# Four transformer layers on one core: layer 1's query product split 3 to 13 heads, and two small steps of each norm moved to VectorE

## The reference

```python
def _layernorm(x, axis=-1, eps=1e-05):
    m = jnp.mean(x, axis=axis, keepdims=True)
    v = jnp.var(x, axis=axis, keepdims=True)
    return (x - m) / jnp.sqrt(v + eps)
...
inter = jnp.einsum('bnchd,bnhde->bnche', q, KVcum)
den_inter = jnp.einsum('bnchd,bnhd->bnch', q, Kcum)
scores = jnp.einsum('bnchd,bnkhd->bnhck', q, k)
scores = jnp.where(mask, scores, 0.0)
intra = jnp.einsum('bnhck,bnkhe->bnche', scores, v)
den_intra = jnp.transpose(jnp.sum(scores, axis=-1), (0, 1, 3, 2))
out = (inter + intra) / (den_inter + den_intra + ATT_EPS)[..., None]
```

## Time and profile before

| | |
|---|---|
| median of 3 runs | 1859.21 us (1857.06 to 1859.85) |
| the profiled execution | 1858.92 us, of which the span of instructions is 1857.1 us |
| PE busy | 1768.9 us, 95% |
| POOL busy | 1273.5 us, 69% |
| DVE busy | 1238.0 us, 67% |
| ACT busy | 1091.2 us, 59% |
| granted TensorE clock | 0.994 of full |

### The profile page before, as it was taken

How to read it: one execution, slowest core, us unless ns; L and a number is a source line. 1 busy time by engine, 2 the same in 40 slices (tenths; PEclk the granted TensorE clock), 3 DMA queues, 4 the chain that set the end, 5 groups by cost and what they waited for, 6 DMA issues and landing times.

```text
span 1857.1 us, 31831 instructions
## 1 busy us (share of the span) xinstructions
PE 1768.9 (95%) x10270; PEld 1340.9 (72%) x10270; DVE 1238.0 (67%) x4307; ACT 1091.2 (59%) x2684; POOL 1273.5 (69%) x1779
## 2 busy tenths in 40 slices
PE   8999999989999999999999899999999999999998
PEld 5788998665666567657665577777778887888874
DVE  7953235687769876887789655543466756768774
ACT  6563225656886578667876676564345556544456
POOL 6665558998879987997899884341356755554465
PEclk9999999999999999999999999999999999999999
DMA  6200000010000000000000000000000001000002
GB/s 237 77 11 1 1 2 4 1 47 1 1 1 1 1 1 1 1 1 1 1 1 1 5 5 5 1 7 1 2 4 1 1 23 26 18 1 1 1 7 63
DMA packets 24473, 26.44 MB, mean 14 GB/s; under 512 B 3492, under 2 KB 21284, under 8 KB 23924
## 3 DMA queue, kind: packets, MB, share of 16 engines
q1 hardware_dynamic: 24308, 24.41, 4.1%
HBM read 22.26 MB, written 2.15 MB: 13 GB/s over the span
## 4 chain that ended last, share of the span: by engine, by line
PE 69%; POOL 14%; DVE 7%; ACT 5%; issue 4%; DMA 0%; POOLq 0%; SPq 0%; DVEq 0%; ACTq 0%
PE ps L86 63%; POOL arena L103 13%; PE ps L89 6%; ACT arena L97 4%; DVE arena L103 2%; DVE arena L109 1%; DVE arena L106 1%; POOL arena L106 1%; DVE arena L126 1%; DVE arena L141 1%; ACT L97 1%; DVE arena L123 0%; DVE arena L129 0%; DVE arena L112 0%; ACT arena L98 0%
## 5 line engine op out<-in xcount | busy, mean ns | idle before, releaser
L103 POOL TENSOR_TENSOR arena<-arena 128x512 f32<-128x512 f32 (+6 forms) x796 | 734.5, 937 | 298.9 <-DVE arena L103 146.5
L97 ACT ACTIVATE arena<-ps 128x128 f32<-128x128 f32 (+9 forms) x1100 | 368.6, 369 | 445.1 <-PE ps L86 337.8
L86 PE MATMUL ps<-arena 128*128 128x128 f32 (+4 forms) x2864 | 465.1, 296 | 25.8 <-DVE arena L103 12.8
L86 PEld LDWEIGHTS ps<-arena 128*128 128x128 f32 x2864 | 380.0, 192 | 118.0 <-issue 47.5
L103 DVE TENSOR_TENSOR arena<-ps,arena 128x128 f32<-128x128 f32 (+4 forms) x680 | 295.0, 446 | 239.3 <-PE ps L86 227.4
L97 ACT ACTIVATE arena<-arena 128x128 f32<-128x128 f32 (+1 forms) x772 | 300.0, 442 | 45.8 <-POOL arena L103 41.3
L97 ACT ACTIVATE arena<-ps,cols 128x512 f32<-128x512 f32 x324 | 216.9, 689 | 170.2 <-PE ps L86 158.1
L86 PE MATMUL ps<-arena,cst 128*128 128x360 f32 (+1 forms) x768 | 294.0, 498 | 17.4 <-POOL arena L103 7.3
L86 PE MATMUL ps<-arena,moe 128*128 128x256 f32 (+1 forms) x960 | 289.8, 441 | 1.4 <-DVE arena L109 0.4
L89 PE MATMUL ps<-cst,arena 128*128 128x128 f32 x1392 | 239.6, 274 | 15.4 <-ACT arena L97 5.1
L103 POOL TENSOR_TENSOR arena<-arena,cst 128x144 f32<-128x144 f32 (+7 forms) x320 | 138.3, 435 | 142.6 <-ACT arena L97 96.6
(11 more groups left out here) (109 smaller groups left out, 1897.6 us busy)
## 6 DMA issues: line engine op xcount, KB each, us to landing
rows<-in_rows SPq DMA_DIRECT2D x1, 2253.0 KB, 15.4
arena<-in_x SPq DMA_DIRECT2D x8, 256.0 KB, 5.0
wf<-in_wf SPq DMA_DIRECT2D x2, 1024.0 KB, 6.5
arena<-in_L_ffn_W SPq DMA_DIRECT2D x8, 256.0 KB, 3.1
out_dram<-arena SPq DMA_DIRECT2D x8, 256.0 KB, 2.5
wmod<-in_wmod SPq DMA_DIRECT2D x4, 384.0 KB, 9.0
arena<-kept SPq DMA_DIRECT2D x24, 64.0 KB, 3.0
arena<-kept SPq DMA_DIRECT2D x8, 192.0 KB, 3.0
```

The lines of the kernel that those rows point to most:

```text
L86: return UNSENT if self.e is None else self.e.matmul(out, lhsT, rhs, start=start, stop=stop)
L97: return self.e.activation(out, in_, func, bias=bias, scale=scale)
L103: return UNSENT if self.e is None else self.e.tensor_tensor(out, a, c, op)
```

## The change

`PARTS` becomes 3, 7 and 6 heads: GpSimd multiplies heads 13 to 15 (216 numbers), VectorE heads 0 to 6 (504) and 7 to 12 (432). ScalarE's copy and the tile `pc` shrink to 216. In each norm the two tensor_scalar instructions move from GpSimd to VectorE, right behind the last aggregate and with a wait for it; GpSimd keeps the power and the product. All four strings of `TURNS` are new, with the same number of digits and the same count of each digit.

```diff
-        self.kv, self.pc = r.take(1152), r.take(360)
+        self.kv, self.pc = r.take(1152), r.take(216)
 TURNS = {
-    "pe": ("0123440000000100011000111000111230002111200022110032013000111220001123300103221100133231112223332221"
...
+    "pe": ("0123440000000000200022000122200012210001110021101322000111300031133300013332001113332222221133311122"
...
 }
         def scales_pool(b, *key, t0=0, t1=NT):
             r = room[b]
             rs, nm = r.rs[:, t0:t1], r.nm[:, t0:t1]
-            rsqrt_pool(b, rs, r.mv[:, t0:t1, 1], EPS, ALU.add, *key)
-            pool.ts(nm, r.mv[:, t0:t1, 0], -1.0, None, ALU.mult).then_inc(*pool.up(b))
+            pool.wait_ge(*at("raw", *key))
+            pool.wait_ge(*pool.last(b))
+            pool.wait_ge(*at("mhalf"))
+            pool.tt(rs, r.shifted[:, t0:t1], mhalf[:, 0:t1 - t0], ALU.pow).then_inc(*pool.up(b, "rsqrt", *key))
             pool.wait_ge(*pool.last(b))
             pool.tt(nm, nm, rs, ALU.mult).then_inc(*pool.up(b, *key))
...
-        def scales(b, *key):
-
-            dve.note(b, "raw", *key)
+        def scales(b, *key, t0=0, t1=NT):
+
+            r = room[b]
+            dve.wait_ge(*dve.last(b))
+            dve.ts(r.shifted[:, t0:t1], r.mv[:, t0:t1, 1], EPS, None, ALU.add).then_inc(*dve.up(b))
+            dve.ts(r.nm[:, t0:t1], r.mv[:, t0:t1, 0], -1.0, None, ALU.mult).then_inc(*dve.up(b, "raw", *key))
             yield
...
-        PARTS = ((11, 16), (0, 6), (6, 11))
+        PARTS = ((13, 16), (0, 7), (7, 13))
...
-                    act.act(m.pc, ps[:, 0:360]).then_inc(*act.up(b, "l1pcopy", b, l, t, free=(b, "l1p", l, t, 11)))
+                    act.act(m.pc, ps[:, 0:216]).then_inc(*act.up(b, "l1pcopy", b, l, t, free=(b, "l1p", l, t, 13)))
...
-                    pool.tt(m.kv4[:, 11:16], m.pc.rearrange("p (h e d) -> p h e d", e=9, d=8), by_e(qk, 11, 16),
+                    pool.tt(m.kv4[:, 13:16], m.pc.rearrange("p (h e d) -> p h e d", e=9, d=8), by_e(qk, 13, 16),
                             ALU.mult).then_inc(*pool.up(b, "l1pc", b, l, t))
```

More of the change, by code:

```diff
@@ new lines @@
+    "act": ("0123444040000200221223122111011003333331421142200030003300100011000002221101030330211000221330220202"
+           "0201300233221220212201022121131311321210112211130311313001212112211121122113333000013100011023032000"
+           "3303301112310000032010300020322303300000201112210222000120332303131113311022220000021201111100200002"
+           "2200122303311123332201223120000031231112223331232130000013133311131032002201223121033311112113222322"
+           "0231333300030013011333113102302220002230221033333113112033000103333110213322122200003222333223301011"
+           "1231102212330003323112111122221032033123111013231000200102223332332111031210000102221112001321323333"
+           "1322220111120100100023223323132121111301100003133302003222322020311133311120232222300000221101113333"
+           "1332011301000301023222223330100033302011111222102000200223110111000101230132301112100010022222011112"
+           "3331000002000213322233313211103323230312221200200021222211112133313003000312101111001132222333231303"
+           "2022222132111133132022223020022031101113233313011123221222303331303000011113013333310322222000313203"
+           "3332233021111113020003203303322223210000211103130210200002222012033300111231002220033200321213022211"
+           "1123210333332122231112112001000222221213211111100300033332132221022311223331111112011003222320212002"
+           "0231000333011030030100110132220111333110200110222130001201012001021300200303333002222030303232333223"
+           "3300221322122113221131331313313333111322211132221332122031102231330011002200033333323020122103330113"
+           "2220311013311033003120331021033331322322022230330321303020330203332012001020112010031122312012012333"
+           "3023133210113021320212302300211031102301110302202132310222303031030021231323132300103002311213120101"
+           "0332213321003133212312031023211020031113112232322101330131100323020301313123220113300223222330102121"
+           "1233313301221103303331123033330120022100023123233200012231331030012331111102303232302101132002013011"
+           "0223022233113330022201303312112210132123301021132322201221201223001303323003123032001332123113011100"
+           "3121132322232210211003223331331103233002213113322230023300022001131111133012221122002200113311300333"
+           "1132223113300002232233323232233"),
@@ L811, in l0_dve @@
                 yield from stats(b, [(r.x[:, t, :], t) for t in range(4 * h, 4 * h + 4)])
-                yield from scales(b, "l0stats", b, h)
+                yield from scales(b, "l0stats", b, h, t0=4 * h, t1=4 * h + 4)
             yield
@@ L999, in moe0_dve @@
                 yield from stats(b, [(r.x[:, t, :], t) for t in range(4 * h, 4 * h + 4)])
-                yield from scales(b, "mstats", b, h)
+                yield from scales(b, "mstats", b, h, t0=4 * h, t1=4 * h + 4)
             yield
@@ L1192, in moe1_dve @@
                 yield from stats(b, [(r.x[:, t, :], t) for t in range(4 * h, 4 * h + 4)])
-                yield from scales(b, "nstats", b, h)
+                yield from scales(b, "nstats", b, h, t0=4 * h, t1=4 * h + 4)
             yield
@@ L1353, in half_stats @@
             yield from stats(b, [(src(t), t) for t in range(4 * g, 4 * g + 4)])
-            yield from scales(b, "l1stats", b, *key)
+            yield from scales(b, "l1stats", b, *key, t0=4 * g, t1=4 * g + 4)
         def half_scales(b, *key):
@@ L1519, in l1_act @@
                     yield
-                    ps = banks.get(b, "l1p", l, t, 11)
-                    act.wait_ge(*at("l1p", b, l, t, 11))
+                    ps = banks.get(b, "l1p", l, t, 13)
+                    act.wait_ge(*at("l1p", b, l, t, 13))
                     if t:
                         act.wait_ge(*at("l1pc", b, l, t - 1))
-                    act.act(m.pc, ps[:, 0:360]).then_inc(*act.up(b, "l1pcopy", b, l, t, free=(b, "l1p", l, t, 11)))
+                    act.act(m.pc, ps[:, 0:216]).then_inc(*act.up(b, "l1pcopy", b, l, t, free=(b, "l1p", l, t, 13)))
                     yield
```

152 lines of the change are left out of this document (81 added, 71 removed).

## The result

The changed kernel takes 1848.04 us (median of 4 runs, 1845.93 to 1850.14) against 1859.2 for the kernel before: a ratio of 0.9942, 95% interval 0.9925 to 0.9959. It is faster by 11 us. The forecast was 10 us slower, and rival A (faster, 1849 us) had 0.3.

What follows compares the result with a forecast made beforehand. PE, 95% busy, bounds the kernel, with GpSimd and VectorE close behind in layer 1. Waits +25 for VectorE, -4 and -5 for GpSimd's relief make +16 us; new orders give 6 back: 1858.9 + 10 = 1869 us, range 1846 to 1888.

Steps and rivals of the forecast that it cites:

- rival A: Layer 1: GpSimd's relief decides and the kernel gets faster, by half of 20 us, to 1849 us; chance 0.3.
- Durations: Attention chunks: GpSimd's product takes 643 ns, ScalarE's copy 345, VectorE's parts 76 ns more each; layer 1 POOL falls to 624 us.
- The blocking: Layer 1 norms: VectorE's SBUF tensor_scalars stand still beside GpSimd work except pow; 0.99 us a pair, 79 us in all.
- What the pair costs and the relief brings: Layer 1: PE's waits for VectorE +25 us, for GpSimd -4, GpSimd-caused waits for others -5; together +16 us.
- What reaches the end: Layer 1's waits add 16 us, the new orders give 6 back: +10 us on the whole kernel.
- no gain or loss of their own: New orders, counted in the strings: same kind as the old, no effect given a number, 6 us allowed either way.
- The law of waits by busy over idle time: Layer 1: PE's waits for an engine follow its busy over idle time; VectorE 3.3 to 8.1, waits 16.9 to 41 us.
- Outside layer 1: Start, mixtures, layers 2 and 3: 40 pairs, covered by PE's idle time or even with GpSimd's saving; nothing.
- The signs: Layer 1: tensor_scalar mean 0.5 us, VectorE 89%, GpSimd 79%; PE over 94.5% favours A, over 5 us outside the order.
- C: Layer 1 norms: the second tensor_scalar of each pair is blocked too; +32 us, 1891 us; chance 0.1.

Runs made afterwards that it cites:

- the crossed runs: Edits and orders recombined: both edits in the old orders 1872.25 us, new orders alone on the kernel before 1894.21 us; each edit alone was also run in both orders.
- nopair_neworder: Changed kernel, new orders, without the two VectorE tensor_scalars of each norm (epsilon and sign left out): 1831.43 us, ratio 0.9843.
- both_oldorder: Both edits (3 and 13 heads, two tensor_scalars of each norm on VectorE) in the four orders of the kernel before: 1872.25 us, ratio 1.0065.

## Why the prediction was wrong

*Durations*: right. 643 ns forecast for GpSimd's product and 642 measured, 676 and 674 for VectorE's longer one, 345 and 348 for the copy. POOL's busy time in layer 1: 624 and 626 us.

*The blocking*: the mechanism was right, and stated in the right direction for both kinds of GpSimd operation. Its size was too large: 0.49 + 0.19 us, less the 0.09 by which they overlap, make 0.59 us a pair, not 0.99, so 47 us in layer 1 in place of 79. The mean of 15 rows of 16 numbers held one of 3.23 us, and the second of a pair is seldom blocked. DVE came to 661 us, not 703.

*What the pair costs and the relief brings*: the waits forecast +25 for VectorE and -9 for GpSimd, +16 together. In the old orders that sum was measured as both edits: +11.8. The two parts of the norm move were measured there too: +24 and -17. The sum came out nearer than its parts, which is partly luck: PE's longest wait, L86 for VectorE, rose by 10.4 us there and not by 25, and that for GpSimd fell by 5.9 and not by 4.

*What reaches the end*: **this step failed, in its last term.** I gave the new orders "a good third back, 6 us", and found "no gain or loss of their own". They gave back 23 us (ratio 1.0065 to 0.9942). Their room for the pair is 5 of these, near the 6; the other 18 are the gain of their own that I put at nothing, measured without the pair (1849.36 to 1831.43). The law of waits by busy over idle time failed with it: with DVE at 84% it would have given 16.9 x (661/129)/3.3 = 26 us of waiting, and the old orders showed 27.3 (DVE at 82%), but the new ones 17.7. Waiting in this kernel is not a function of load. It is load against the order: in the orders laid for the new durations PE waits for VectorE hardly longer than before, though the pair still costs 17 us; with the old durations the same orders cost 34 us. That the fit of order and durations decides is shown by the crossed runs; which turns make it is open. Counting where the elements leave a stage says nothing about that fit.

*Outside layer 1* I put nothing. The edits alone indeed change nothing there: in the old orders the differences of each edit and of both stand when 60% of PE's columns are done, and stay within 1 us. But 5 to 6 us of the changed kernel's 11 arise behind that point. By the same working the new orders alone gain 2.6 us there, and with the short product 3.0; with GpSimd's short norms they gain 5.7 in the changed kernel and 5.7 to 7.5 in the others (3.7 with the pair twice). So the larger gain needs the new orders and the short norms together; which turn makes it was not tried.

*The signs* that I had named were there: PE's busy share in layer 1 rose over 94.5%, to 95.0% (750.53 of 790 us), and more than 5 us came outside it. Those for the blocking held in part: the tensor_scalars of a pair took 0.34 us in the mean, where I gave 0.5 and 0.2 as the bound; GpSimd came to 79%, as forecast, but VectorE to 84% and not 89%, and PE's waits for it to 17.7 us and not towards 40.

*The rivals.* A's time was right (1849) and its reason in part: GpSimd left the chain, from 26% to under 6%. But in the old orders the relief lost against the pair, as forecast, so A was decided by the orders, which it did not speak of: that its time came out is luck. C, the second operation blocked too, is out: 2 of 72, and 7 of 67 with both edits in the old orders.

## What to carry to other kernels

When an edit comes with a new hand-laid order, the order is the larger unknown: here each of the two alone made the kernel slower (+12 and +34 us) and together faster by 11, so a forecast from durations alone should stay wide on both sides, and an experiment should cross edit and order before it judges either. And small VectorE tensor_scalars from SBUF to SBUF beside a busy GpSimd cost far more than their length; the same arithmetic as a tensor_reduce gave back 13 us of 17 here.

## What the runs showed of the hardware that I had not expected

- A tensor_scalar of 4 or 8 numbers waits as one of 16 does (up to 1.97 us in the changed kernel), and when GpSimd's operations follow on each other it can lose the turn again and again: 3.87 us behind five of them.
- The second of two tensor_scalars with no wait between them was seldom held up, in 2 of 72 pairs in the changed kernel and 7 of 67 with both edits in the old orders: it starts 0.09 us before the first ends, and the row at 428.89 shows both done in 2.02 us behind one block of 1.96.
- A pow on GpSimd, 1.0 us long, holds no tensor_scalar up: 0.24 us for a pair inside it. In all 17 traces 255 tensor_scalars of 4, 8 or 16 numbers began inside a pow, and none took over 0.22 us; of 567 that began inside another GpSimd operation, with 0.16 us or more of it to go, 536 took over 0.23. The rule of the Trainium skill's SBUF — State Buffer (Who interferes with whom), by which any GpSimd instruction would hold them up, goes too far there.
- A reciprocal or a tensor_reduce of 4 or 8 numbers at the same place is not held up (means of 147 to 177 ns).
- PE's busy time is not a constant of its work: from 1756.2 us (nopair_neworder, granted clock 0.996) to 1779.3 (both_oldorder, 0.991) for the same 10270 records.
